# Transformer layer with two expert mixes: id copies one tile sooner, the list wait behind tile 34's loads, and one addition a tile later

## The reference

```python
h = tok(x)                                  # 16x16 patches of 32 images -> 192 columns, class token, positions
h = concatenate([h, txt], axis=1)           # 32 x 274 rows of 192
h = h + attention(layernorm(h))             # 12 heads, rotary, causal
h = h + ffn(layernorm(h))
# ffn, over all N = 8768 rows:
pc = softmax(h @ Wsc + bsc); route_c = argmax(pc); pmax_c = max(pc)
dropped = rank of the row within its expert, by falling pmax_c, >= N / 4
common  = W2c[e] applied to gelu(h @ W1c[e] + b1c[e]) + b2c[e],  e = route_c       # 192 -> 768 -> 192
pu = softmax(h @ Wsu + bsu); route_u = argmax(pu)
unique  = the same with the other four experts, e = route_u
out = common + dropped * unique
```

## Time and profile before

| what | value |
|---|---|
| median of 3 runs | 1224.29 us (1220.61 to 1225.76) |
| the profiled execution | 1224.32 us, its span 1222.6 us |
| busy share of the span | PE 91%, PEld 81%, DVE 71%, POOL 61%, ACT 52% |
| chain that ended last | PE 14% of the span, POOL 7%, issue 6%, DVE 3%, DMA 1% |
| of which by line | h_ps L1967 6%, y_ps L1978 6%, list_d L185 4%, out_dram L1866 3% |

### The profile page before, as it was taken

How to read it: one execution, slowest core, us unless ns; L and a number is a source line. 1 busy time by engine, 2 the same in 40 slices (tenths; PEclk the granted TensorE clock), 3 DMA queues, 4 the chain that set the end, 5 groups by cost and what they waited for, 6 DMA issues and landing times. The chain is left out here.

```text
span 1222.6 us, 33890 instructions
## 1 busy us (share of the span) xinstructions
PE 1112.7 (91%) x12830; PEld 994.6 (81%) x12830; DVE 867.0 (71%) x1925; ACT 634.6 (52%) x1154; POOL 742.5 (61%) x1190
## 2 busy tenths in 40 slices
PE   3889999999999999999999998768999999998983
PEld 3768888888878878878878887558999999998983
DVE  7567778788788788888888788557997754444341
ACT  2245565565556556546556555445545555554540
POOL 6445556555765765765675673543563777776575
PEclk8789999999999999999999999779999999999997
DMA  6101112213323322422322321287986777777641
GB/s 212 46 24 55 54 44 69 65 44 105 116 67 99 119 71 82 126 80 77 119 93 62 118 83 53 97 287 279 311 304 231 229 263 275 250 242 259 215 165 33
DMA packets 84805, 168.71 MB, mean 138 GB/s; under 512 B 16622, under 2 KB 57877, under 8 KB 84640
## 3 DMA queue, kind: packets, MB, share of 16 engines
q1 hardware_dynamic: 70976, 140.50, 35.5%
q0 software_dynamic: 13664, 26.00, 6.1%
HBM read 124.45 MB, written 45.45 MB: 139 GB/s over the span
## 5 line engine op out<-in xcount | busy, mean ns | idle before, releaser
L903 ACT ACTIVATE PT<-round_banks 128x1752 f32<-128x1752 f32 x96 | 156.8, 1633 | 111.4 <-PE round_banks L687 111.4
L2050 ACT ACTIVATE Gl<-h_ps,W 128x256 f32<-128x256 f32 x264 | 116.0, 474 | 165.4 <-PE h_ps L1967 156.5
L1978 PE MATMUL y_ps<-W,Gl 128*128 128x192 f32 x1056 | 183.3, 328 | 0.0
L1978 PEld LDWEIGHTS y_ps<-W,Gl 128*128 128x128 f32 x1056 | 172.9, 191 | 0.0
L1967 PE MATMUL h_ps<-XH,Wh 128*128 128x256 f32 x528 | 147.0, 296 | 12.0 <-DVE Wl L2116 5.1
L1074 POOL TENSOR_SCALAR_AFFINE_SELECT PT<-PT 128x512 f32<-128x512 f32 x192 | 118.0, 641 | 61.6 <-ACT PT L903 61.0
L1212 DVE TENSOR_TENSOR capped<-round_banks,masks_f 128x1024 f32<-128x1024 f32 x96 | 117.3, 1222 | 35.0 <-PE round_banks L660 34.6
L569 PE MATMUL gen<-w_emb,xh 128*128 128x192 f32 (+1 forms) x768 | 124.9, 270 | 18.0 <-POOL xl L1003 13.1
L1967 PE MATMUL h_ps<-XH,Wl 128*128 128x256 f32 x528 | 139.7, 286 | 0.0
L569 PEld LDWEIGHTS gen<-w_emb,xh 128*128 128x128 f32 (+1 forms) x768 | 102.5, 167 | 24.9 <-issue 20.8
L1866 POOL DMA_INDIRECT out_dram<-Y,sid x76 | 83.5, 1099 | 64.4 <-DVE Y L2140 33.3
(11 more groups left out here) (298 smaller groups left out, 2761.5 us busy)
## 6 DMA issues: line engine op xcount, KB each, us to landing
W<-in_experts_dram SPq DMA_DIRECT2D x44, 771.0 KB, 5.0
W<-in_experts_dram SPq DMA_DIRECT2D x44, 672.0 KB, 5.8
xT<-in_xT_dram SPq DMA_DIRECT2D x32, 591.0 KB, 4.2
X<-sorted_d SPq DMA_DIRECT2D x35, 386.0 KB, 3.8
stage<-rows_d SPq DMA_DIRECT2D x64, 192.0 KB
rows_d<-h SPq DMA_DIRECT2D x32, 192.0 KB, 3.7
out_dram<-h SPq DMA_DIRECT2D x32, 192.0 KB, 6.4
rows_d<-xn SPq DMA_DIRECT2D x32, 192.0 KB, 2.0
```

The source lines that it names most:

```text
L903: act.activation(PT[(JG * b + j) % 2][:], R[:, :, 0:438], ACT.Exp, scale=SCALE).then_inc(exps, 1)
L1978: mm = pe.matmul(y_ps[t.par][:, k * D:(k + 1) * D], Gl[t.par][:, f, k * P:(k + 1) * P], W[t.i][:, W2O + f * D:W2O + (f + 1) * D], start=(f ...
L2050: act.activation(Gl[t.par][:, f, :], h_ps[f % 3][:, 0:ROWS], ACT.Gelu, bias=W[t.i][:, B1O + f:B1O + f + 1]).then_inc(g_ready, 1)
```

## The change

Three things move, and no instruction is added or removed.

1. On POOL, `number` runs one tile sooner: in body(t) for tile t-1 and ahead of `send(t-3)`, where it ran for tile t-2 and behind it.
2. On SP, the wait for all list scatters and the first two list loads stand in body(34) behind tile 34's loads, where they stood in body(33).
3. On DVE, `add_rest(37)` stands in body(41), where it stood in body(40).

```diff
@@ SP
-                    if t.number == FIXED - 2:
+                    if t.number == FIXED - 1:
 
                         sp.wait_ge(spread_out, 16 * COLS)
-                        for n in range(FIXED, FIXED - 2 + AHEAD):
+                        for n in range(FIXED, FIXED - 1 + AHEAD):
                             load_list(static(n))
-                    if t.number is not None and FIXED - 2 <= t.number < STATIC - AHEAD:
+                    if t.number is not None and FIXED - 1 <= t.number < STATIC - AHEAD:
                         load_list(static(t.number + AHEAD))
@@ POOL
+                if t.number is not None and 1 <= t.n < FIXED + 1:
+                    number(t.before(1))
                 if t.number is None:
                     cast(t)
                     gather(t)
...
-                if t.number is not None and 2 <= t.n < FIXED + 2:
-                    number(t.before(2))
@@ DVE
-                    if t.number in (FIXED + 1, CT, CT + 2):
-                        add_rest(static({FIXED + 1: FIXED, CT: CT - 2, CT + 2: CT - 1}[t.number]))
+                    if t.number in (FIXED + 1, CT, CT + 3):
+                        add_rest(static({FIXED + 1: FIXED, CT: CT - 2, CT + 3: CT - 1}[t.number]))
```

## The result

| | before | after |
|---|---|---|
| median, 20 runs each | 1225.49 us (1218.55 to 1232.66) | 1229.2 us (1222.62 to 1234.88) |
| ratio to before | | 1.004, 95% interval 1.0024 to 1.0057 |
| the profiled execution, and its span | 1224.32, 1222.6 us | 1226.84, 1225.1 us |

The kernel got slower, by about 4 to 5 us. The profiled execution of after is one of its faster runs, 2.4 us under its median.

What follows compares the result with a forecast made beforehand. The prediction took a chain of waits through POOL's list and result scatters to bound the kernel. From 1224.32 us it took 9.0 for an earlier send(34) and added 5.6 for tile 37's late addition: 1220.9 us, range 1218.5 to 1223.

Steps and rivals of the forecast that it cites:

- List stage: Tiles of body(16) to body(31): ids one tile sooner bring 7.95 us a tile instead of 8.23, gaining 3.8 us.
- first rival: POOL's meetings with DVE's `Wl` stay, the list stage gives POOL nothing: 1224.5 us, chance 0.18.
- the list ids of tile 35 then reach POOL at 1102.1 - 3.8 = 1098.3: End of the list stage: tile 35's list ids reach POOL 3.8 us sooner than the 1102.1 of before.
- PE waits 0.1 to 2.7 us: At turn(35), due at 1106.4: PE waits this long for tile 35's gather, landing 3.7 to 6.3 us after its start.
- cast(35) to send(34): POOL's stretch of DMA issues and casts, 30.88 us before, takes 25.5 us; send(34) comes 9.0 us sooner, bounds 11 and 4.
- Send(34) to the addition of tile 36: POOL's own issues and two landings after send(34): nothing moves, so the chain shifts by the same 9.0 us.
- third rival: Tile 35's scatter lands at the median, so its 6.58 us wait may be 3.9 shorter: 1217.0 us, chance 0.15.
- Tile 37's addition: DVE's addition behind add_bias(40) reaches POOL 7.0 us late, making the end 5.6 us later, bounds 4.5 and 7.0.
- Sum: Whole kernel: 1224.32 - 9.0 + 5.6 = 1220.9 us, from the profiled execution of before.
- slower rival: At turn(35), tile 35's gather becomes the wait, send(34) only 3.6 us sooner: 1226.3 us, chance 0.12.

Runs made afterwards that it cites:

- hold 36: Moves 1 and 2 of the change, plus an SP wait holding tile 36's weights until tile 35's gather has landed: 1217.28 us, 0.9936 of before.
- both holds: Moves 1 and 2, with SP holding tile 36's weights until tile 35's gather landed and tile 40's until tile 35's scatter landed: 1216.99 us, 0.9938 of before.
- hold 40: SP holds tile 40's weights until tile 35's result has landed; ratio to before 0.9981 on before, 0.9942 on move 1, 0.9991 on after.

## Why the prediction was wrong

**List stage: right in its size, by another way.** 7.94 us a tile were measured for 7.95 forecast, 4.4 us for 3.8 (bounds 0 and 4.5). Down(14) to down(31) took 135.89 us, forecast 135.15. The tile taken as undisturbed (7.93) was not: its id copy took 0.41 us instead of 0.22 beside a `Wl`, and the tile before it (1073.58 to 1081.30) took 7.72. POOL alone is thus 0.2 us faster than PE and DVE, runs into a `Wl` once in each tile, is held for 0.22 us, and so keeps the pace of 7.94. The meetings stayed, as the first rival says, but one small one a tile, and without the price of that rival. The pace of before is not fixed by its order either: move 3's trace had 141.8 us. The Trainium skill (SBUF — State Buffer, section "SBUF: two separate sides") has an exclusive lock of the shared ports behind that rival; the trace agrees in that POOL was held, by 0.2 us a tile, while that `Wl` kept its 0.96 us.

**The first step that failed: "the list ids of tile 35 then reach POOL at 1102.1 - 3.8 = 1098.3".** It let the last list scatter land as before, while the same edit put tile 34's loads around it: 1.16 MB within 1.4 us ahead of its start, and 0.67 MB 0.2 us behind it. From the last list scatter to cast(35) took 9.89 us in after and 8.63 with moves 1 and 2, for 6.21 before. That gives back 3.7 or 2.4 of the 4.4. Shown by taking the loads away: 3.05 with nothing ahead, 4.92 with the rows, 6.7 to 8.1 with up weights and rows.

**The second: "PE waits 0.1 to 2.7 us" for tile 35's gather**, from the landing times of the gathers in before. It waited 5.7 to 6.6 us in all four traces with move 2 and no hold 36, and its next down pass was slow in each (5.11 to 5.79 us). So cast(35) to send(34) took 28.78 us (29.29 without move 3) instead of the 25.5 to 25.7 forecast. Hold 36 showed that tile 36's weights make the landing late, and that the forecast of POOL's own work was near: 24.6, and 25.7 with both holds. Tile 36's weights are not all of the wait, though. The sum had the gather's second half start 4.5 us behind cast(35) (1102.8 - 1098.3); it started 6.5 behind in after and with hold 36, and 7.1 in before (1102.10 to 1109.21). An idle time of some 2 us between the two scatters of tile 30, in before's trace too, had been left out. With hold 36, and the late list ids still there, PE waited 1.42 us, inside the forecast.

The two together, for send(34): 4.4 - 3.7 + 2.1 = 2.8 us sooner in after, and 4.4 - 2.4 + 1.6 = 3.6 with moves 1 and 2, where 9.0 was forecast and 4 was its lower bound. The forecast had looked at what stands behind the wait on SP's queue, and not at what the freed loads lie beside.

**Send(34) to the addition of tile 36: wrong in the trace, and by chance.** The third rival had seen the weight load that lies beside tile 35's scatter, and was held unlikely because "the same chain" releases both. But tile 40's weights and the scatter go out 0.2 us apart, and their order decides 5 us. After's trace had the short wait (third rival), that of moves 1 and 2 the long one.

**Tile 37's addition: right in kind and place**, a wait of 9.33 us at send(37) released by DVE and none in front of send(38). Its price depends on the case above, which I hadn't seen. With the short wait the tail grew by 5.9 us (82.1 against 76.2) and with hold 40 by 5.4 (81.6 against 76.2), near the 5.6 forecast. With the long one it grew by 7.7 (88.4 against 80.7). The nearness is in part luck: send(37) came 8.3 us later behind send(34) with the short wait and 9.0 with the long one, not the 7.0 forecast, and the gap in front of send(38) that swallows a part is 2.6 with the short wait and the forecast's 1.3 with the long one.

**Sum.** With the long wait: 1225.49 - 3.6 + 7.7 = 1229.6 us against the 1229.2 measured. By these terms, of the 8.3 us between forecast and median about 5.4 are the gain that wasn't there, 2.1 the price of the addition, and the rest how the profiled execution of before stood to its median. This fits and does not prove: the terms are from single traces, after's own 2.8 in place of 3.6 would give 1230.4, and in move 3's trace, with its quick list stage in the old order, send(34) came at 177.6, 5 us sooner than in before.

The slower rival, tile 35's gather, was the right mechanism at 0.12. That its 1226.3 us lie near the profiled 1226.84 is luck. The profiled execution of after is 2.5 us longer than that of before because its first list scatter comes 4.0 later, which is the scatter between executions, send(34) 2.8 sooner, and the tail, with the short wait, is 1.4 longer.

## What to carry to other kernels

When an edit frees a large load, ask which small transfer on the critical path it will now be issued beside, and price that transfer's landing anew: a landing time from the old trace holds only with its old neighbours. Where two queues issue within a fraction of a microsecond of each other, look for two outcomes in several traces, and settle the order by a wait on the load that has slack. A combined change should be taken apart early: here the first move was worth about 3 us (by its interval 0 to 5.5), the second nothing that can be told, and the third cost 6 to 8.

## What the runs showed of the hardware that was not expected

- A POOL scatter or gather of small rows landed late when SP issued 1.1 to 1.8 MB of loads around it, and soon when it didn't: POOL's wait 6.4 to 6.8 against 1.4 us for tile 35's scatter, PE's 5.8 against 1.42 us for its gather, 6.7 to 8.1 against 3.05 us for the last list scatter. At tile 40 it was the order that counted: 0.2 us ahead of the second half was late in five traces of five, 0.4 us behind its end early in three of three.
- Weights issued 3.6 us ahead of a gather did no such harm: in hold 36, tile 35's weights went out at 1103.99 and the halves of the gather at 1107.60 and 1108.96.
- Most stops of PE cost more than themselves. Behind 6.57 us in after the next down pass took 5.11 us instead of 4.08, and the mean granted clock was 0.72 over 12 us. Behind 4.07 us (move 1) the pass took 6.61, and behind 2.15 us (holds 36 and 40) 5.33. Behind 1.42 us (hold 36) and 2.42 us (move 3) it stayed at 4.08.
- A two-input VectorE operation held up POOL's issues in the list stage: a scatter that began 0.35 us before the end of a `Wl` took 1.19 us instead of 0.97, in each of 16 tiles, and so POOL kept the pace of PE and DVE.
